# Strassen's products for the gate and up projections of MLP chunks 3 to 6, and another order at the start of the first head group

## The chip, the cores and the metric

The kernel runs on one core of a Trainium2 chip. The metric is device time in microseconds (us), as a median of three runs. TensorE (PE) does the matrix products, VectorE (DVE), ScalarE (ACT) and GpSimd (POOL) the elementwise work, and SyncE (SP) issues the transfers. Each engine works through its own instructions in order and waits on semaphores that the others raise.

## The reference

A decoder layer on x of 8 x 128 tokens of width 512, all in float32: a Mamba-2 block, then a gated MLP of inner width 1792, a layer norm, cross attention with 32 query heads in 8 groups, a layer norm, a mixture of low-rank adapters, and a last layer norm. The change touches the MLP,

```
h2 = rmsnorm(h, ln2_w)
mlp = silu(h2 @ gate_w.T) * (h2 @ up_w.T) @ down_w.T
```

and the start of the cross attention, `q = rmsnorm(x @ Wq.T)`, `k = rmsnorm(ctx @ Wk.T)`, softmax of `q k`, times `v`, times `Wo`.

## The kernel before

**Split operands.** A float32 operand is kept as two float32r parts, hi (a copy that ACT makes) and lo (the operand less hi, a subtraction by POOL for weights and by DVE for most activations). `mm3` (L509 to 513) makes each product of three matmuls: hi with hi, hi with lo, lo with hi. A 128 x 512 piece of output with K = 512 takes four K blocks, so 12 matmuls.

**The MLP.** The inner width is cut into seven chunks of 256 (c = 0 to 6; chunk 3 of the title is c = 2). Activations `act_hi` and `act_lo` lie transposed, 512 x 1024 tokens. A chunk has four steps `gu_step` (m = 0 to 3: two halves of 128 rows for each of two halves of 512 tokens), each with a gate product and an up product, 24 matmuls, into PSUM banks 2, 3 or 4, 5. Then:

- ACT: `silu` of the gate bank into `sg` (L1235).
- DVE: `hb = sg * up bank` (L2163). It waits until POOL has read the `hb` of two steps earlier (`hlo_done`), and PE starts a step only when the `hb` of two steps earlier is made (`h_done`).
- ACT: `h_hi` (L1243). POOL: `h_lo`.

After the four steps PE does eight down projections `dn_step` (one of 128 tokens each, 6 matmuls, banks 6 and 7). The first four need `h_lo` of steps 0 and 1, the last four that of steps 2 and 3 (`hlo_done`); from the third on each waits until DVE has added the bank of two earlier to the residual (`add_res` L2049, `o_add`). The hi and lo of the next chunk's gate and up weights (four pieces of 128 x 512: ACT `gu_hi` L1199, POOL `gu_rest`, through `lo` L1580) are made under the down projections. SP loads 1024 KB of them into `raw_a` when `gu_l` says that the old ones are split, and 512 KB of down weights into `raw_b`. All seven chunks have this form; chunks 2 to 5 are a loop on every engine.

Chunk 0 also holds the last norms and transposes (13 to 15). Chunk 1 holds six pieces of the context's split (ACT `ctx_split`, DVE `ctx_rest` through `lo` L1942, two behind each of the first three multiplications) and eight additions of x to the residual on POOL (`add_x` L1698: two, three and three behind `h_lo` 0, 1 and 2).

**The first head group.** Its slots take one block of 128 tokens each. The query projection of the next group is made by Strassen's seven products (`q_prod` L781, one in each slot) over the two halves of K and of the tokens, with sums of weights (POOL `combine_s`) and of tokens: t1, t2, t3, t4 are made raw, then hi by ACT (`t_round` L1342) and lo by DVE (`t_rest`). PE waits for the lo of a token sum by `t_lo`: product 1 for t3, product 2 for t2, product 3 for t1. In slot 1 DVE does `ot_rest`, `t_rest(t2)` and then `q_part`, which feeds the matmul `fold` of slot 2 (L806). Slot 0 begins on PE with `kv_step`, `s_step(0, 1)`, `q_step(1, 1)`.

The order of all this is written out by hand: each engine's program is a list of such calls.

Of the kernel before, what the change touches and what calls it, by code (L numbers as in the profile page):

```python
# [13 lines left out]
P = 128  # L14
# [15 lines left out]
def build_program(nc, x, ctx_t, mask, consts, fold_in, chan, rows, w_dt, w_in, w_out, w_gu, w_dn,  # L30
# [9 lines left out]
    with ctx:  # L40
# [76 lines left out]
        with ExitStack() as m:  # L117
            h_hi = sb(m, "h_hi", [P, 2, B * L], f32r)
            h_lo = sb(m, "h_lo", [P, 2, B * L], f32r)
            sg = sb(m, "sg", [P, 2, NTOK])  # L120
            hb = sb(m, "hb", [P, 2, NTOK])
            xre = sb(m, "xre", [P, B, DM])


        with ExitStack() as m:
# [30 lines left out]
            qpart = sb(m, "qpart", [P, 2, GH * 16])  # L156
            q2 = sb(m, "q2", [P, NTOK])
# [15 lines left out]
        t4_raw = [xn[:, k, :] for k in range(2)]  # L173
        p1_s = [w_raw[:, 0, 3072 + m * 512:3584 + m * 512] for m in range(2)]
# [76 lines left out]

        block = ctx.enter_context(nc.Block())
# [8 lines left out]
        WP_COL = [1024, 1536]  # L261
        A11, A12, A21, A22 = 0, 1, 2, 3
# [65 lines left out]
        def wo_turn(g, h):  # L328

            return 4 * g + ((h + 1) % 4 if is_last(g) else h) + 1  # L330

# [42 lines left out]
        def _(sp_eng):  # L374
# [48 lines left out]
            def next_mlp(c):  # L423

                sp_eng.wait_ge(dn_l, 2 * c + 2)
                sp_eng.dma_start(raw_b[:, 0:1024], w_dn[bass.ds(c + 1, 1)].rearrange("a p n -> (a p) n"))\
                    .then_inc(ld_dn, 16)
                sp_eng.wait_ge(gu_l, 4 * c + 4)
                sp_eng.dma_start(raw_a[:, :], w_gu[bass.ds(c + 1, 1)].rearrange("a p n -> (a p) n"))\
                    .then_inc(ld_gu, 16)  # L430

# [13 lines left out]
            with sp_eng.Fori(1, MLP_IT - 1) as c:  # L445
                next_mlp(c)

            sp_eng.wait_ge(gu_l, 4 * MLP_IT)
# [57 lines left out]
        def _(pe):  # L506
# [161 lines left out]
            def gu_step(c, k, n, turn=None):  # L668

                m_i = 2 * n + k  # L670
                pe.wait_ge(gu_l, 4 * c + 2 * k + 2)
                if not (isinstance(c, int) and 4 * c + m_i < 2):
                    pe.wait_ge(h_done, 4 * c + m_i - 1)
                tok = slice(n * NTOK, (n + 1) * NTOK)
                for which in range(2):
                    if which and turn is not None:
                        norm_t(turn, tb)
                    o = bank[(2, 4)[m_i % 2] + which]
                    for kk in range(KT):
                        c0 = GU_COL + (2 * k + which) * 512 + kk * P  # L680
                        t = mm3(o[:, :], w_hi[:, c0:c0 + P], w_lo[:, c0:c0 + P],
                                act_hi[:, kk, tok], act_lo[:, kk, tok], kk == 0, kk == KT - 1)
                t.then_inc(gu_mm, 1)

# [63 lines left out]
            with pe.Fori(2, MLP_IT - 1) as c:  # L748
                mlp_step(c)
# [114 lines left out]
            def slot(g, jj, make=True, before=True):  # L864
# [3 lines left out]
                turn = (g, jj + 1) if j < 3 else (pg, 4 * pn)  # L868
                if j == 3:
# [7 lines left out]
                if not before:  # L877
                    q_step(1, 1)
# [139 lines left out]
        def _(act):  # L1018
# [173 lines left out]
            def gu_hi(c, i):  # L1192

                act.wait_ge(ld_gu, 16 * c + 16)
                if isinstance(c, int) and c == 0:
                    act.wait_ge(in_mm, 20)
                else:
                    act.wait_ge(gu_mm, 4 * c)
# [32 lines left out]
            def silu(c, m_i):  # L1231
                act.wait_ge(gu_mm, 4 * c + m_i + 1)
# [20 lines left out]
            def mlp_step(c):  # L1253
# [23 lines left out]
                if not last:  # L1277
# [13 lines left out]
            def wq_hi(x):  # L1291
                act.wait_ge(ld_q, 16)
                act.wait_ge(*((o_mm, 8) if x < 2 else (gu_mm, 4 * MLP_IT)))
# [23 lines left out]
            with act.Fori(2, MLP_IT - 1) as c:  # L1317
                mlp_step(c)
# [68 lines left out]
            def slot(g, jj, make=True):  # L1387
# [46 lines left out]
                if start and jj == 0:  # L1434
                    wp_hi(1, 1)
                if start and jj == 1:
# [5 lines left out]
                part = part_late(g, jj)  # L1442
                if part and (make or jj < 3):
                    d, qn, qh = part
                    q_square(g + d, qn, qh)
# [129 lines left out]
        def _(pool):  # L1575
# [92 lines left out]
            def gu_rest(c, i):  # L1668
                pool.wait_ge(gu_h, 4 * c + i + 1)
# [30 lines left out]
            def mlp_step(c):  # L1700
                second, last = (isinstance(c, int) and c == x for x in (1, MLP_IT - 1))
                for m_i in range(4):
# [7 lines left out]
                    if second and m_i < 3:  # L1710
                        for b in ((0, 1), (2, 3, 4), (5, 6, 7))[m_i]:
                            add_x(b)
                    if last and m_i == 1:
# [4 lines left out]
                if not last:  # L1718
# [89 lines left out]
            with pool.Fori(2, MLP_IT - 1) as c:  # L1808
                mlp_step(c)
# [120 lines left out]
        def _(dve):  # L1930
# [225 lines left out]
            def mlp_step(c):  # L2156
                first, second, last = (isinstance(c, int) and c == x for x in (0, 1, MLP_IT - 1))
                for m_i in range(4):
                    dve.wait_ge(silu_done, 4 * c + m_i + 1)
                    dve.wait_ge(gu_mm, 4 * c + m_i + 1)  # L2160
# [13 lines left out]
                    if second and m_i < 3:  # L2174
                        ctx_rest(2 * m_i + 2)
                        ctx_rest(2 * m_i + 3)
                for b in range(B):
# [12 lines left out]

            mlp_step(0)
            mlp_step(1)
            with dve.Fori(2, MLP_IT - 1) as c:
                mlp_step(c)
# [128 lines left out]
            def slot(g, jj, make=True, before=True):  # L2323
# [51 lines left out]
                if start and jj == 1:  # L2375
                    t_rest(t2, t2_raw, 2, t_step, 12)
                if start and jj == 2:
                    t_rest(t1, t1_raw, 4, t_step, 8)
                if start and jj == 4:
                    t_rest(t4, t4_raw, 6, t_step, 14)  # L2380
                part = part_late(g, jj)
                if part and (make or jj < 3):
                    d, qn, qh = part
                    q_part(g + d, qn, qh)

# [229 lines left out]
```

## Time and profile before

| | |
|---|---|
| Median of three runs | 989.66 us (987.52 to 990.65) |
| Profiled execution | 986.14 us, of which 984.0 us are its span |
| MLP | about 133 to 364 us of the span |
| First head group begins | about 390 us |

Times in the rows count from the span's start. In a row of a timeline stand the start, the length, the engine, the line, what is written and read, the number of instructions, and in brackets how long the engine was idle before and what ended that. PE's matmuls overlap: the distance of two starts is what one costs, the length is its latency.

### The profile page before, as it was taken

What the parts mean: (1) busy time and instruction counts of PE and PEld (TensorE: products, weight loads), DVE (VectorE), ACT (ScalarE), POOL (GpSimd) and SP (SyncE); (2) the same over time, 40 slices, a digit from 0 to 9 for tenths busy, and PEclk for the clock granted to TensorE, in tenths of its full rate; (3) what the DMA queues carried; (4) which work ended last, traced back from release to release, by engine and by line L of the source; (5) the groups of instructions that cost most, each with busy time, mean ns of one, the idle gap of its engine ahead of it and who ended that gap; (6) DMA issues with size and microseconds to landing.
All of it is one profiled execution on the core that took longest, in us unless ns stands there. A gap on an engine that the chain in (4) does not pass through costs nothing.

```text
span 984.0 us, 15661 instructions
## 1 busy us (share of the span) xinstructions
PE 947.5 (96%) x4926; PEld 784.7 (80%) x4926; DVE 639.6 (65%) x1421; ACT 486.9 (49%) x1358; POOL 523.7 (53%) x432
## 2 busy tenths in 40 slices
PE   5998999999999999989999999999999999999896
PEld 3765688788888888878888888888888888888782
DVE  5755553513221357889778778768768778778877
ACT  5666442412231246645644654745645645555554
POOL 4346623834343456864674673673673764854323
PEclk9999999999999999999999999999999999999996
DMA  6200022310111111010110110110110120110002
GB/s 222 84 3 31 13 89 86 107 65 0 64 64 64 45 64 36 23 44 22 44 52 15 43 53 11 43 53 11 43 62 2 43 64 0 45 52 12 1 1 85
DMA packets 18024, 45.69 MB, mean 46 GB/s; under 512 B 2176, under 2 KB 2816, under 8 KB 16704
## 3 DMA queue, kind: packets, MB, share of 16 engines
q1 hardware_dynamic: 17984, 45.20, 13.7%
q8 instruction: 20, 0.33, 0.1%
q14 instruction: 20, 0.16, 0.1%
HBM read 43.10 MB, written 2.10 MB: 46 GB/s over the span
## 4 chain that ended last, share of the span: by engine, by line
PE 77%; POOL 7%; DVE 7%; issue 4%; ACT 2%; DMA 2%; SPq 0%; POOLq 0%; DVEq 0%; ACTq 0%
PE bank L511 22%; PE bank L513 22%; PE bank L512 22%; PE bank L828 4%; PE bank L838 2%; POOL w_lo L1580 2%; DMA raw_a<-in_w_q 1%; DVE pb L2299 1%; POOL res L1698 1%; PE bank L522 1%; POOL pb L1837 1%; PE bank L815 1%; POOL raw_a L1742 1%; PE bank L597 1%; DVE bst L2129 1%
## 5 line engine op out<-in xcount | busy, mean ns | idle before, releaser
L511 PE MATMUL bank<-act_hi,w_hi 128*128 128x512 f32 x448 | 182.7, 408 | 1.6 <-DVE act_lo L1942 1.6
L513 PE MATMUL bank<-act_hi,w_lo 128*128 128x512 f32 x448 | 175.3, 391 | 0.0
L512 PE MATMUL bank<-act_lo,w_hi 128*128 128x512 f32 x448 | 175.1, 391 | 0.0
L1837 POOL TENSOR_TENSOR pb<-pb,prec 128x512 f32<-128x512 f32 x64 | 66.8, 1044 | 163.1 <-DVE prec L2308 163.1
L1580 POOL TENSOR_TENSOR w_lo<-raw_a,w_hi 128x512 fp32r<-128x512 f32 x101 | 130.2, 1301 | 37.1 <-ACT w_hi L1302 21.6
L1371 ACT ACTIVATE pb<-pb,nmax 128x128 f32<-128x128 f32 x256 | 99.4, 391 | 46.5 <-DVE nmax L2303 46.5
L511 PE MATMUL bank<-w_hi,ot_hi 128*128 128x512 f32 x256 | 106.2, 415 | 1.1 <-DVE ot_lo L1942 0.6
L1580 POOL TENSOR_TENSOR h_lo<-hb,h_hi 128x512 fp32r<-128x512 f32 x28 | 37.3, 1333 | 120.5 <-ACT h_hi L1243 120.5
L511 PEld LDWEIGHTS bank<-act_hi,w_hi 128*128 128x128 f32 x448 | 84.7, 189 | 20.2 <-issue 4.1
L513 PE MATMUL bank<-w_hi,ot_lo 128*128 128x512 f32 x256 | 100.5, 393 | 0.0
L512 PE MATMUL bank<-w_lo,ot_hi 128*128 128x512 f32 x256 | 100.2, 391 | 0.0
L512 PEld LDWEIGHTS bank<-act_lo,w_hi 128*128 128x128 f32 x448 | 84.7, 189 | 18.0 <-issue 2.2
L513 PEld LDWEIGHTS bank<-act_hi,w_lo 128*128 128x128 f32 x448 | 84.4, 188 | 18.0
L2163 DVE TENSOR_TENSOR hb<-sg,bank 128x512 f32<-128x512 f32 x28 | 19.3, 688 | 115.8 <-ACT sg L1235 115.8
L1379 ACT ACTIVATE pt_hi<-bank 128x512 fp32r<-128x512 f32 x64 | 38.3, 598 | 105.5 <-PE bank L838 105.5
L1235 ACT ACTIVATE sg<-bank 128x512 f32<-128x512 f32 x28 | 16.8, 599 | 130.3 <-PE bank L513 130.3
L1580 POOL TENSOR_TENSOR w_lo<-raw_b,w_hi 128x512 fp32r<-128x512 f32 x56 | 72.1, 1306 | 7.1 <-ACT w_hi L1039 7.1
L511 PE MATMUL bank<-w_hi,ctx_hi 128*128 128x256 f32 x256 | 72.7, 284 | 0.0
L2299 DVE SCALAR_TENSOR_TENSOR pb<-bank,qr,mask_sb 128x128 f32<-128x128 f32 x256 | 71.5, 342 | 1.3 <-POOL qr L1825 1.2
L513 PE MATMUL bank<-w_hi,ctx_lo 128*128 128x256 f32 x256 | 71.6, 280 | 0.0
L512 PE MATMUL bank<-w_lo,ctx_hi 128*128 128x256 f32 x256 | 71.4, 279 | 0.0
L828 PE MATMUL bank<-k_t,q_t 128*128 128x128 f32 x512 | 67.7, 275 | 0.9 <-DVE pb L2299 0.8
(233 smaller groups left out, 2330.1 us busy)
## 6 DMA issues: line engine op xcount, KB each, us to landing
raw_a<-in_w_gu SPq DMA_DIRECT2D x7, 1024.0 KB, 5.3
raw_a<-in_w_q SPq DMA_DIRECT2D x28, 256.0 KB, 3.3
raw_b<-in_w_kv SPq DMA_DIRECT2D x8, 512.0 KB, 3.2
raw_b<-in_w_dn SPq DMA_DIRECT2D x7, 512.0 KB, 3.3
raw_b<-in_w_o SPq DMA_DIRECT2D x7, 512.0 KB, 4.9
raw_a<-in_w_o SPq DMA_DIRECT2D x14, 256.0 KB, 3.8
res<-in_x SPq DMA_DIRECT2D x8, 256.0 KB, 5.4
raw_b<-in_ctx_t SPq DMA_DIRECT2D x8, 256.0 KB, 3.0
```

The source lines that it names most:

```text
L511: mm(o, l_hi, r_hi, start=first, stop=False)
L512: mm(o, l_hi, r_lo, start=False, stop=False)
L513: return mm(o, l_lo, r_hi, start=False, stop=last)
L828: t = mm(bank[3][:, h * L:(h + 1) * L], q_t[:, n, h, tok], k_t[:, n, tok], start=True, stop=True)
L838: t = nc.tensor.transpose(bank[4][:, h * L:(h + 1) * L], pb[:, jj % 2, h, :], ident)
L1235: A(sg[:, m_i % 2, :], bank[(2, 4)[m_i % 2]][:, :], ACT.Silu).then_inc(silu_done, 1)
L1371: t = A(pb[:, jj % 2, h, :], pb[:, jj % 2, h, :], ACT.Exp, bias=nmax[:, jj % 2, h:h + 1], accum_out=psum_[:, jj % 2, h:h + 1])
L1379: A(pt_hi[:, :], bank[4][:, :], ACT.Copy).then_inc(pthi_done, 1)
L1580: TT(dst, src, f32(hi), ALU.subtract).then_inc(done, 1)
L1837: TT(pb[:, jj % 2, :, :], pb[:, jj % 2, :, :], prec[:, jj % 2, :].unsqueeze(2).to_broadcast([P, GH, L]), ALU.mult).then_inc(p_norm, 1)
L2163: TT(hb[:, m_i % 2, :], sg[:, m_i % 2, :], bank[(3, 5)[m_i % 2]][:, :], ALU.mult)\
L2299: t = STT(pb[:, jj % 2, h, :], bank[3][:, h * L:(h + 1) * L], qr[:, 4 * n + h, j:j + 1], mask_sb[:, :], ALU.mult, ALU.add)
```

## The change

- The four pieces of gate and up weights of a chunk are stored by halves of K: A11 and A12 (gate, K halves), A21 and A22 (up). Each `gu_step` of the chunks 0, 1 and 6 waits for all four.
- In chunks 2 to 5 PE makes seven products of 12 matmuls. Product 0 of a chunk stands ahead of the down projections of the chunk before. Banks are 2 to 5, 0 and 1.
- POOL makes four sums of weights for each of these chunks, and the lo of seven pieces in place of four. The second load of a chunk's weights (768 KB) waits for the lo of the last piece of the chunk before (`gl(c) + 7`).
- DVE makes 14 additions of a product to a running sum for each of these chunks; the multiplications read SBUF alone.
- The token sums t3 and g1 are made by POOL in chunk 0 (`gate_t3` behind the down weights' lo, `gate_t1` behind `h_lo` 2), t2 and half of t4 by DVE in chunk 1, and the rest in chunk 2.
- At the start of the first head group `q_square` (ACT) and `q_part` (DVE) stand ahead of the splits of token sums, `t_rest(t2)` goes to slot 2, and `q_step(1, 1)` goes to the head of slot 0.

In the diff, calls that follow one another are joined on a line, and words in brackets at the right are added.

```diff
+        def gl(c): 4 * c below c = 2, else 7 * c - 6        (gu_l, gu_h: weights split)
+        def gm(c): 4 * c below c = 2, else 14 * c - 20      (gu_mm: products done)
...
+            def next_fast(c):                               (SP)
+                sp_eng.wait_ge(gs_done, 4 * c + 4)
+                sp_eng.wait_ge(gu_l, gl(c) + 1)
+                load_g(c + 1)
+                sp_eng.wait_ge(dn_l, 2 * c + 2)
+                load_dn(c + 1)
+                sp_eng.wait_ge(gu_l, gl(c) + 7)
+                load_g_rest(c + 1)
...
-                pe.wait_ge(gu_l, 4 * c + 2 * k + 2)         (PE, gu_step)
+                pe.wait_ge(gu_l, gl(c) + 4)
...
+            def gate_prod(c, i):
+                pe.wait_ge(gu_l, gl(c) + i + 1)
+                if i == 0:
+                    pe.wait_ge(*((h_done, 8) if isinstance(c, int) and c == 2 else (ga_done, 12 * c - 22)))
+                elif i == 1:
+                    pe.wait_ge(h_done, 4 * c)
+                elif i == 3:
+                    pe.wait_ge(gc_done, 2 * c + 6)
+                elif i > 3:
+                    pe.wait_ge(ga_done, 12 * c - 14 + {4: 0, 5: 2, 6: 6}[i])
+                if isinstance(c, int) and c == 2 and i in (1, 2, 3, 6):
+                    pe.wait_ge(gt_lo, {1: 12, 2: 12, 3: 14, 6: 16}[i])
+                for m in range(2):
+                    for k in range(2):
+                        c0 = GU_COL + i % 4 * 512 + (2 * m + k) * P
+                        b_hi, b_lo = gate_rhs(i, k)
+                        t = mm3(bank[G_PAIR[i][m]][:, :], w_hi[:, c0:c0 + P], w_lo[:, c0:c0 + P], b_hi, b_lo,
+                                k == 0, k == 1)
+                    t.then_inc(gu_mm, 1)
+            def mlp_fast(c, more=True):
+                for i in range(1, 7):
+                    gate_prod(c, i)
+                if more:
+                    gate_prod(c + 1, 0)
+                for b in range(B):
+                    dn_step(c, b)
...
+                if not before:                              (PE, head of slot)
+                    q_step(1, 1)
...
+            def mlp_fast(c, more=True):                     (ACT)
+                A(gp1[m], bank[G_PAIR[0][m]][:, :], ACT.Copy).then_inc(gc_done, 1)     (m = 0, 1)
+                gb_hi(c, 4); dn_hi(c, 0); gb_hi(c, 5); dn_hi(c, 1); gb_hi(c, 6)
+                silu_fast(c, 0); silu_fast(c, 1); gb_hi(c + 1, 0)
+                h_split(c, 0); h_split(c, 1); silu_fast(c, 2); silu_fast(c, 3); gb_hi(c + 1, 1)
+                h_split(c, 2); h_split(c, 3); gb_hi(c + 1, 2); gb_hi(c + 1, 3)
...
+                    if first and m_i == 0:                  (POOL, mlp_step)
+                        gate_t3()
+                    if first and m_i == 2:
+                        gate_t1()
+            def gate_t3():                                  (gate_t1 alike: six operations)
+                for k in range(2):
+                    g_op(t3_raw[k], b21[k][1], b11[k][1], ALU.subtract, 0)
+                for k in range(2):
+                    g_op(t3_raw[k], t3_raw[k], b21[k][0], ALU.add, 9 + k)
+                for k in range(2):
+                    g_op(t3_raw[k], t3_raw[k], b11[k][0], ALU.subtract, 11 + k)
+            def gate_s(c):
+                pool.wait_ge(ld_g11, 16 * c)
+                pool.wait_ge(ld_gu, 16 * c + 16)
+                TT(gu_block(2), quad(A11), quad(A21), ALU.subtract).then_inc(gs_done, 1)
+                pool.wait_ge(gs_done, 4 * c + 1)
+                TT(gu_block(1), quad(A22), gu_block(2), ALU.subtract).then_inc(gs_done, 1)
+                TT(gu_block(3), quad(A21), quad(A22), ALU.add).then_inc(gs_done, 1)
+                TT(gu_block(4), quad(A12), gu_block(1), ALU.subtract).then_inc(gs_done, 1)
+            def mlp_fast(c, more=True):
+                gb_rest(c, 4); dn_rest(c, 0); gb_rest(c, 5); dn_rest(c, 1); gb_rest(c, 6)
+                gate_s(c + 1); gb_rest(c + 1, 0)
+                h_rest(c, 0); h_rest(c, 1); gb_rest(c + 1, 1)
+                h_rest(c, 2); h_rest(c, 3); gb_rest(c + 1, 2); gb_rest(c + 1, 3)
...
                     if second and m_i < 3:                  (DVE, mlp_step)
                         ctx_rest(2 * m_i + 2)
                         ctx_rest(2 * m_i + 3)
+                        if m_i == 0:
+                            gate_t2(0)
+                        elif m_i == 1:
+                            gate_t2(1)
+                            gate_lo(t3, t3_raw, 0)
+                        else:
+                            gate_t4(0)
+                            gate_lo(t2, t2_raw, 2)
...
+            def mlp_fast(c):                                (each gate_adds: 2 additions, of i = 3: 4)
+                for i in range(1, 5):
+                    gate_adds(c, i)
+                gate_mul(c, 0); gate_mul(c, 1); gate_adds(c, 5); gate_adds(c, 6)
+                gate_mul(c, 2); gate_mul(c, 3)
+                for b in range(B):
+                    add_res(8 + 8 * c + b, b, 6 + b % 2)
...
-                if start and jj == 1:                       (DVE, slot)
-                    t_rest(t2, t2_raw, 2, t_step, 12)
                 part = part_late(g, jj)
                 if part and (make or jj < 3):
                     d, qn, qh = part
                     q_part(g + d, qn, qh)
+                if start and jj == 2:
+                    t_rest(t2, t2_raw, 2, t_step, 12)
+                    t_rest(t1, t1_raw, 4, t_step, 8)
```

## Rows read from the trace of the kernel before

**Rows 1.** The page, part 1: busy time, share of the span, instructions.

```profile
PE 947.5 (96%) x4926; PEld 784.7 (80%) x4926; DVE 639.6 (65%) x1421; ACT 486.9 (49%) x1358; POOL 523.7 (53%) x432
```

**Rows 2.** Busy time by stretch, chunks 2 and 5: stretch, length, engines, PEclk, DMA share, GB/s.

```profile
200.50:233.20 32.70, 32.70 (x145) 26.99 (x145) 8.26 (x12) 8.05 (x14) 12.67 (x10) 1.00 0.13 49
...
298.70:331.50 32.80, 32.80 (x146) 27.08 (x145) 8.26 (x12) 8.05 (x14) 12.69 (x10) 1.00 0.16 55
```

**Rows 3.** The timeline of PE inside a gate product.

```profile
170.08 0.39 PE L512 MATMUL bank<-act_lo,w_hi 128*128 128x512 f32 x1
170.31 0.39 PE L513 MATMUL bank<-act_hi,w_lo 128*128 128x512 f32 x1
```

**Rows 4.** The timeline of POOL in chunk 0.

```profile
142.33 2.54 POOL L1580 TENSOR_TENSOR w_lo<-raw_b,w_hi 128x512 fp32r<-128x512 f32 x2
...
158.41 1.30 POOL L1580 TENSOR_TENSOR h_lo<-hb,h_hi 128x512 fp32r<-128x512 f32 x1 [4.14 <-ACT h_hi L1243]
159.66 5.06 POOL L1580 TENSOR_TENSOR w_lo<-raw_a,w_hi 128x512 fp32r<-128x512 f32 x4
```

**Rows 5.** The timeline of ACT, end of chunk 0: silu, h_hi, weights' hi.

```profile
156.34 0.60 ACT L1235 ACTIVATE sg<-bank 128x512 f32<-128x512 f32 x1 [2.41 <-PE bank L513]
157.70 0.63 ACT L1243 ACTIVATE h_hi<-hb 128x512 fp32r<-128x512 f32 x1 [0.76 <-DVE hb L2163]
```

**Rows 6.** The timeline of DVE in chunk 1.

```profile
176.35 3.28 DVE L1942 TENSOR_TENSOR ctx_lo<-raw_b,ctx_hi 128x512 fp32r<-128x512 f32 x2 [2.26 <-ACT ctx_hi L1250]
...
181.45 1.14 DVE L1942 TENSOR_TENSOR ctx_lo<-raw_b,ctx_hi 128x512 fp32r<-128x512 f32 x1 [1.22 <-ACT ctx_hi L1250]
...
189.72 0.69 DVE L2163 TENSOR_TENSOR hb<-sg,bank 128x512 f32<-128x512 f32 x1 [0.79 <-ACT sg L1235]
...
191.91 0.69 DVE L2049 TENSOR_TENSOR res<-res,bank 128x512 f32<-128x512 f32 x1 [0.69 <-PE bank L513]
...
196.92 0.69 DVE L2049 TENSOR_TENSOR res<-res,bank 128x512 f32<-128x512 f32 x1 [1.58 <-PE bank L513]
```

**Rows 7.** The timeline of POOL in chunk 1, beside the first row above.

```profile
176.08 3.00 POOL L1580 TENSOR_TENSOR w_lo<-raw_b,w_hi 128x512 fp32r<-128x512 f32 x2
```

**Rows 8.** DVE, first head group: two operations on SBUF with nothing like them on POOL.

```profile
429.19 1.28 DVE L1942 TENSOR_TENSOR act_lo<-act_raw,act_hi 128x512 fp32r<-128x512 f32 x2
```

**Rows 9.** The page, part 6: issues, KB each, median us to landing.

```profile
raw_a<-in_w_gu SPq DMA_DIRECT2D x7, 1024.0 KB, 5.3
...
raw_b<-in_w_dn SPq DMA_DIRECT2D x7, 512.0 KB, 3.3
```

**Rows 10.** The timeline of PE around the fold of slot 2.

```profile
424.92 0.43 PE L806 MATMUL bank<-qpart,fold 128*128 128x64 f32 x2 [2.54 <-DVE qpart L2220]
...
427.68 0.78 PE L511 MATMUL bank<-t,w_hi 128*128 128x512 f32 x1
428.25 0.61 PE L512 MATMUL bank<-t,w_hi 128*128 128x512 f32 x1
428.68 0.42 PE L513 MATMUL bank<-t,w_lo 128*128 128x512 f32 x1
```

**Rows 11.** Busy time by stretch: after that idle time, and after another.

```profile
82.00:86.00 4.00, 3.95 (x16) 2.67 (x15) 2.49 (x4) 3.83 (x9) 3.77 (x4) 1.00 0.00 0
...
425.00:429.00 4.00, 3.84 (x13) 3.06 (x14) 3.93 (x11) 3.04 (x8) 1.41 (x2) 0.57 0.00 0
```

**Rows 12.** PE's idle time ahead of the first of those stretches.

```profile
81.05 0.67 PE L597 MATMUL bank<-att,xtok 128*128 128x512 f32 x1 [2.12 <-DVE yb L2043]
```

**Rows 13.** The timeline of DVE in slots 1 and 2.

```profile
414.74 0.69 DVE L1942 TENSOR_TENSOR ot_lo<-bank,ot_hi 128x512 fp32r<-128x512 f32 x1 [0.64 <-ACT ot_hi L1385]
417.05 2.36 DVE L1942 TENSOR_TENSOR t<-t_raw,t 128x512 fp32r<-128x512 f32 x2 [1.62 <-POOL xn L1793]
...
424.18 0.69 DVE L2220 TENSOR_REDUCE qpart<-q2t 128x16 f32<-128x512 f32 x1
...
428.58 0.69 DVE L1942 TENSOR_TENSOR ot_lo<-bank,ot_hi 128x512 fp32r<-128x512 f32 x1
```

**Rows 14.** The timeline of PE in slot 0.

```profile
393.02 1.13 PE L828 MATMUL bank<-k_t,q_t 128*128 128x128 f32 x8 [0.75 <-DVE pb L2299]
```

More of the change, by code:

```diff
@@ L1276, in mlp_step @@
                         wkv_hi(0, 1)
-                if not last:
+                    if second and m_i == 0:
+                        t_round_g(t3, t3_raw, gt_pool, 13)
+                    if second and m_i == 2:
+                        t_round_g(t2, t2_raw, gt_dve, 15)
+                if first:
+                    for i in range(4):
+                        gu_hi(1, i)
+                if second:
+                    gb_hi(2, 0)
+                    gb_hi(2, 1)
+                    act.wait_ge(x_add, 8)
+                    t_round_g(g1, g1_raw, gt_pool, 19)
+                    gb_hi(2, 2)
+                    gb_hi(2, 3)
@@ new lines, in silu_fast @@
+            def silu_fast(c, x):
+                m, n = x % 2, x // 2
+                act.wait_ge(ga_done, 12 * c - 10 + 2 * n + m + 1)
+                gate = (gu2, gp1)[n][m]
+                A(gate, gate, ACT.Silu).then_inc(silu_done, 1)
+            def mlp_fast(c, more=True):
+                peeled = isinstance(c, int) and c == 2
+                for m in range(2):
+                    act.wait_ge(gu_mm, gm(c) + m + 1)
+                    act.wait_ge(h_done, 4 * c)
+                    if peeled:
+                        act.wait_ge(x_add, 8)
+                    A(gp1[m], bank[G_PAIR[0][m]][:, :], ACT.Copy).then_inc(gc_done, 1)
+                gb_hi(c, 4)
+                dn_hi(c, 0)
+                gb_hi(c, 5)
+                dn_hi(c, 1)
+                gb_hi(c, 6)
+                if peeled:
+                    act.wait_ge(cx_l, 8)
+                    t_round_g(t4, t4_raw, gt_dve, 19)
+                silu_fast(c, 0)
+                silu_fast(c, 1)
+                if more:
+                    gb_hi(c + 1, 0)
+                h_split(c, 0)
+                h_split(c, 1)
+                silu_fast(c, 2)
+                silu_fast(c, 3)
+                if more:
+                    gb_hi(c + 1, 1)
+                h_split(c, 2)
+                h_split(c, 3)
+                if more:
+                    gb_hi(c + 1, 2)
+                    gb_hi(c + 1, 3)
+                else:
@@ L1700, in mlp_step @@
             def mlp_step(c):
-                second, last = (isinstance(c, int) and c == x for x in (1, MLP_IT - 1))
+                first, second, last = (isinstance(c, int) and c == x for x in (0, 1, MLP_IT - 1))
                 for m_i in range(4):
@@ L1717, in mlp_step, with g_op, gate_t3 @@
                         wkv_rest(0, 1)
-                if not last:
+                if first:
+                    for i in range(4):
+                        gu_rest(1, i)
+                if second:
+                    gate_s(2)
+                    for i in range(4):
+                        gb_rest(2, i)
+            def g_op(o, x, y, op, seen):
+                if seen:
+                    pool.wait_ge(gt_pool, seen)
+                TT(o, x, y, op).then_inc(gt_pool, 1)
+            def gate_t3():
+                pool.wait_ge(n_lo, 12)
+                for k in range(2):
+                    g_op(t3_raw[k], b21[k][1], b11[k][1], ALU.subtract, 0)
+                for k in range(2):
+                    g_op(t3_raw[k], t3_raw[k], b21[k][0], ALU.add, 9 + k)
+                for k in range(2):
+                    g_op(t3_raw[k], t3_raw[k], b11[k][0], ALU.subtract, 11 + k)
```

224 lines of the change are left out of this document (186 added, 38 removed).

## The prediction

> **What bounds the kernel now.** I read the page's first part, then the busy time by stretch, then the timelines of the MLP engine by engine. PE is busy for 96% of the span [rows 1]. In chunks 2 and 5 it is busy for the whole stretch, at PEclk 1.00, and the two between are alike; POOL works 12.7 of 32.7 us there, DVE 8.3 [rows 2]. A chunk is 96 + 48 = 144 matmuls in 32.75 us, so one costs 0.227 us, which is the distance of two starts [rows 3] and not the 0.39 us of a record. So PE's instruction count sets the time, as long as nobody makes PE wait; the question is whether the added work does.
>
> **What goes.** Seven products of 12 matmuls replace 96: 12 fewer in each of four chunks, 48 x 0.227 = 10.9 us off PE.
>
> **What comes, unit prices.** A POOL operation on 128 x 512 costs 1.26 us in a row of four (5.06 / 4) [rows 4]. ACT takes 0.60 to 0.63 [rows 5]. DVE takes 0.69 where one input is a PSUM bank [rows 6], whatever POOL does. With both inputs in SBUF it takes 0.64 while POOL rests (1.28 / 2) [rows 8], but 1.64 beside POOL (3.28 / 2) [rows 6], and POOL's two then take 3.00 in place of 2.54: each such DVE operation holds POOL up by 0.46 [rows 4, 7]. It looks as if they take turns: DVE waits for the POOL operation in progress. A lone one takes 1.14 [rows 6].
>
> The Trainium skill says so in so many words ("SBUF — State Buffer", section "SBUF: two separate sides"): the port pair is an exclusive lock, held for a whole instruction, against DVE operations with two SBUF inputs. The trace agrees (1.64 against 0.64). By that rule every sum that the change puts on DVE while POOL has a queue costs one POOL operation more; by the row of a resting POOL it would be free of this, which is the first rival.
>
> **Chunk 0 (POOL's sums).** The lo of the down weights ends at 144.9 [rows 4]. Then `gate_t3` takes 6 x 1.26 = 7.6 (to 152.4), `h_lo` 1 and 2 take 2.5 (155.0), `gate_t1` 7.6 (162.5), the two context subtractions of DVE hold it up by 2 x 0.46 (163.4), and `h_lo` 3 ends at 164.7 instead of 159.7. PE ends its products at 156.3 [rows 5] and wants `h_lo` 3 for the fifth down projection, 4 x 6 x 0.229 = 5.5 later, at 161.8. So PE stands for 2.9 us; behind it are four down projections and all of chunk 1. The lo of chunk 1's weights (5.06 from 164.7) is ready at 169.8 while PE ends at 170.2, so the wait for all four pieces costs nothing more. Everything is now 2.8 us late. Bounds: 2.0 if DVE's two don't disturb, 3.5.
>
> **Chunk 1 (DVE's sums and splits).** DVE's context subtractions grow from 6 to 16 operations on SBUF: four behind the first multiplication, six behind the second, six behind the third, and the next multiplication stands behind them. POOL has 3, 4 and 4 operations in these stretches. In the chunk's new time:
> - The first block begins at 176.35 + 2.8 = 179.15, takes 4 x 1.64 = 6.6, and the second multiplication ends at 186.4.
> - Then ACT rounds h and a piece of context, a gap of 1.3 (1.22 in [rows 6]), then four operations beside POOL and two without: 6.6 + 1.3; the third multiplication ends at 196.2.
> - The same again: the fourth ends at 206.1, against 190.4 + 2.8 = 193.2.
> - DVE's first additions to the residual come after it; the third down projection waits for the first of them, to 206.8. Some first operations of a block come free at once (the 1.14), so I take 0.9 off: 205.9.
>
> PE would begin that third projection at 191.9 + 2.8 = 194.7, where its second ends (in the kernel before DVE's second addition starts at 191.91) [rows 6]. It stands for 11.2 us, with six projections behind it. In the kernel before, it waited 0.9 there for POOL (1.58 in place of 0.69 between two additions [rows 6]); that goes. Net 10.3. Bounds: with 0.64 for all 16 it is 0 (the blocks fit into a step of 5.4), with 1.64 for all 12.5.
>
> **Chunks 2 to 5 (the handover to the next chunk's product 0).** PE reaches it after six products: 6 x 12 x 0.227 = 16.3 us after product 1 begins. What it waits for: product 2 ends at 5.4; ACT's hi and POOL's lo of piece 6 take 0.63 + 1.26, with the hand-overs 7.6. Only then SP issues 768 KB; 512 KB land in 3.3 us and 1024 KB in 5.3 [rows 9], so 4.3: 11.9. Then POOL makes four sums and the lo of the piece, 5 x 1.26 = 6.3: 18.2, and DVE's two multiplications, which now read SBUF alone, hold it up by 0.9: 19.1. PE stands for 2.8 us; queued behind are product 0 and eight down projections. `h_lo` 0 to 3 follow at POOL in time. Three handovers have this (2 to 3, 3 to 4, 4 to 5). The first is later by 0.8, because POOL comes late out of chunk 1 and DVE has six more operations on SBUF. Sum 9.2. Bounds: 0.2 each (a load that lands after 2.7, and no lock) to 4.4. DVE's 14 additions, 0.69 each, fit between the products (2.7 for 2 or 4 of them), and ACT's 19 operations too.
>
> **PE's clock.** After 2.54 us without work (and 0.16 more) the matmul starts lie 0.43 apart until 428.7 [rows 10]; PEclk is 0.57 over 425 to 429, half clock (1.2 of 2.4 GHz) for 3.4 us [rows 11], a loss of 1.7. After 2.12 us idle [rows 12] it stayed at 1.00 [rows 11]. The five new waits are 2.9, 11.2, 3.6, 2.8, 2.8. The long one surely pays 1.7; I give the four others 0.7 each, between 0 and 1.7. Sum 4.5; bounds 0 and 8.5.
>
> The Trainium skill describes this case ("TensorE: Matmul & The Clock Gate", section "HAM oscillation — how this bites in real kernels"): a loop that waits in each round drops the clock in each round. By it all five pay, 8.5 and not 4.5, the third rival; the row of 2.12 us speaks against it for the short ones.
>
> **Start of the first head group.** `q_part` no longer stands behind `t_rest(t2)`: it can follow `ot_rest` (ends 415.4) where it followed the split (ends 419.4) [rows 13], so the fold's 2.54 us go. But `t_rest(t2)` is now behind `ot_rest` of slot 2, and product 2 waits for it. Moved forward by the 3.9 us that DVE gains, `ot_rest` stands at 424.7 in place of 428.58, and t2's lo is ready at 425.3 + 1.28 = 426.6. PE, without the fold's wait and at full clock, is there at 423.5: it stands for 3.1 us in the next place, and its clock falls there as before. It began product 2 at 427.68 [rows 10] and begins it at 426.6, but runs more of it at half clock. I take -0.5; bounds 0 and -5 (no new wait). In slot 0 PE's 0.75 us go [rows 14], but `kv_step` 1 still waits for DVE's copy of k; 0, bounds 0 and -0.7.
>
> **The sum**, against the profiled 986.14 us: -10.9 + 2.9 + 10.3 + 9.2 + 4.5 - 0.5 = +15.5, so 1001.6. That execution was 3.5 us below the median of 989.66; from the median it is 1005.2. I predict 1005.
>
> **Rivals.**
> 1. *POOL and DVE keep ahead: faster.* The place is the shared path of POOL and DVE; the price is the 0.46 and 1.0 of each meeting. It decides at 0.64 us for DVE's operations on SBUF: then chunk 1 has no stop, each handover costs 1.8 and chunk 0 costs 2.0: -10.9 + 2.0 - 0.9 + 5.4 - 0.5 = -5.0, about 985. For it: DVE is busy only 65% and POOL 53% [rows 1]. Against it: the 1.64 beside POOL. Chance 0.11.
> 2. *The pile-up in chunk 1 is half of mine*, because DVE's operations meet POOL less: at the lone 1.14 to 1.2 in place of 1.64, 12 operations give back 5.5, and a shorter wait is kinder to the clock: +9, about 999. Chance 0.17.
> 3. *The clock falls at each wait*: +4 more, about 1009. Chance 0.14.
> 4. My forecast: 0.52. Between the first two lies a rest of 0.06, in which the sums cancel (about 990), from handovers that land early.
>
> The likeliest's own range is 1000 to 1011. The range of 8 in 10 is 992 to 1013: it takes in the second and the third. A measurement of this kernel tells 0.3% (3 us) from no change. Faster than 986.7: 0.11; within: 0.06; slower than 992.6: 0.83.
>
> **What would show it.** On PE's timeline: a stop ahead of the fifth down projection of chunk 0 (released by `h_lo`); one of about 11 us ahead of the third of chunk 1 (by DVE's addition to the residual); one at each product 0, released by `w_lo`, with POOL's first weight sum right behind the landing of the load; DVE's subtractions and sums in chunk 1 at 1.6 us each; PEclk below 1.00 behind the waits; and at the head group a wait at product 2 in place of the fold's. My forecast falls if DVE's 16 operations take under 1 us each, or if the 768 KB land before 10 us after product 1 begins.

## The result, and the profile after

The changed kernel takes 1010.35 us (median of 4, 1006.07 to 1014.53), the kernel before beside it 989.53: ratio 1.021, interval 1.019 to 1.023, so it is slower, by about 2%. Predicted were 1005 us, range 992 to 1013. The profiled execution took 1008.71 us, against 986.14; its sum was predicted as 1001.6. I count chunks from 0, as the prediction does.

The page's part 1 of the kernel after, to [rows 1]: POOL worked 56 us more, DVE 59 us more, and PE has 48 matmuls fewer. PE's busy time is the same to 0.1 us all the same: from the start of the MLP to that of the first head group it is 3.1 us less, where half clock and a longer pitch (the distance of two starts) take back most of what the 48 matmuls gave, and before the MLP it is 3.0 us more (below).

```profile
PE 947.4 (94%) x4878; PEld 781.0 (78%) x4878; DVE 698.6 (69%) x1493; ACT 501.6 (50%) x1386; POOL 580.1 (58%) x472
```

PE's waits of the kernel after over 120 to 400 us (the MLP; what PE waited for: us in total, times, longest):

```profile
PE bank L563 <- DVE res L2297: 11.6, 3, 11.0
PE bank L563 <- POOL w_lo L1743: 9.6, 3, 3.5
PE bank L563 <- POOL h_lo L1743: 2.8, 1, 2.8
```

And where they stand, in PE's timeline (start, length, then the idle time before it). In order: the fifth down projection of chunk 0, the third of chunk 1, product 0 at three handovers, the fold and product 2 of the first head group, which answer to [rows 10]:

```profile
167.63 0.50 PE L563 MATMUL bank<-w_hi,h_hi 128*128 128x512 f32 x1 [2.75 <-POOL h_lo L1743]
...
209.38 0.76 PE L563 MATMUL bank<-w_hi,h_hi 128*128 128x512 f32 x1 [11.02 <-DVE res L2297]
...
242.69 0.50 PE L563 MATMUL bank<-act_hi,w_hi 128*128 128x512 f32 x1 [3.45 <-POOL w_lo L1743]
...
276.45 0.49 PE L563 MATMUL bank<-act_hi,w_hi 128*128 128x512 f32 x1 [3.08 <-POOL w_lo L1743]
...
310.16 0.79 PE L563 MATMUL bank<-act_hi,w_hi 128*128 128x512 f32 x1 [3.07 <-POOL w_lo L1743]
...
445.23 0.33 PE L899 MATMUL bank<-qpart,fold 128*128 128x64 f32 x2
...
450.11 0.76 PE L563 MATMUL bank<-t,w_hi 128*128 128x512 f32 x1 [3.37 <-issue]
```

Look at the lengths too: a record of 0.76 to 0.79 behind a wait is a matmul at half clock, one of 0.47 to 0.50 at full clock. The stretches say the same (start:end, length, PE busy, PEclk, DMA share, GB/s):

```profile
204.00:212.00 8.00, 2.62 (x6) 0.50 0.00 0
...
310.00:316.00 6.00, 5.84 (x14) 0.50 0.00 0
...
276.00:284.00 8.00, 7.55 (x33) 1.00 0.10 33
```

DVE in chunk 1, to [rows 6]. The pairs L2451 and L2458 are token sums beside POOL's additions; L2190 `t<-t_raw,t` is a low part while POOL rests. After them the additions to the residual (L2297) come, on which PE waited 11.02. The last line is POOL's, two additions of x beside the first pair: 1.72 each, where 1.26 is its price undisturbed:

```profile
185.69 3.48 DVE L2451 TENSOR_TENSOR t_raw<-t_raw,act_hi 128x512 f32<-128x512 f32 x2
...
190.98 3.07 DVE L2190 TENSOR_TENSOR ctx_lo<-raw_b,ctx_hi 128x512 fp32r<-128x512 f32 x2 [1.22 <-ACT ctx_hi L1343]
193.97 3.49 DVE L2451 TENSOR_TENSOR t_raw<-t_raw,act_lo 128x512 f32<-128x512 f32 x2
197.39 1.28 DVE L2190 TENSOR_TENSOR t<-t_raw,t 128x512 fp32r<-128x512 f32 x2
...
203.43 3.41 DVE L2458 TENSOR_TENSOR xn<-act_hi,t_raw 128x512 f32<-128x512 f32 x2
...
208.56 1.27 DVE L2297 TENSOR_TENSOR res<-res,bank 128x512 f32<-128x512 f32 x2
```

```profile
185.17 3.44 POOL L1861 TENSOR_TENSOR res<-res,xre 128x512 f32<-128x512 f32 x2
```

POOL at the first handover: it sits idle until the load lands, then makes the weight sums and only then the low part for which PE waits (L1743 at 241.36):

```profile
236.09 1.50 POOL L1925 TENSOR_TENSOR w_raw<-raw_a 128x512 f32<-128x512 f32 x1 [5.80 <-DMA raw_a<-in_w_gu]
...
240.14 1.27 POOL L1930 TENSOR_TENSOR w_raw<-raw_a,w_raw 128x512 f32<-128x512 f32 x1
241.36 1.27 POOL L1743 TENSOR_TENSOR w_lo<-raw_a,w_hi 128x512 fp32r<-128x512 f32 x1
242.58 2.55 POOL L1743 TENSOR_TENSOR h_lo<-hb,h_hi 128x512 fp32r<-128x512 f32 x2
```

### The profile page after: what moved, and what is told of

Same layout as the page of the kernel before. It is cut to its first block, busy times and chain, and to the rows that moved or that the text cites. A ratio compares the mean times of both kernels' runs of the same rounds, so it can differ in the third digit from the quotient of the medians.

```text
span 1006.9 us, 15750 instructions
## 1 busy us (share of the span) xinstructions
PE 947.4 (94%) x4878; PEld 781.0 (78%) x4878; DVE 698.6 (69%) x1493; ACT 501.6 (50%) x1386; POOL 580.1 (58%) x472
## 4 chain that ended last, share of the span: by engine, by line
PE 72%; POOL 8%; DVE 8%; issue 5%; DMA 2%; ACT 2%; SPq 0%; POOLq 0%; DVEq 0%; ACTq 0%
PE bank L563 21%; PE bank L565 20%; PE bank L564 20%; PE bank L921 4%; POOL w_lo L1743 3%; PE bank L931 2%; DMA raw_a<-in_w_q 1%; PE bank L574 1%; DVE pb L2629 1%; POOL t_raw L1897 1%; PE bank L624 1%; DVE t_raw L2451 1%; PE bank L908 1%; PE bank L649 1%; DVE bst L2377 1%
## 5 line engine op out<-in xcount | busy, mean ns | idle before, releaser
L563 PE MATMUL bank<-act_hi,w_hi 128*128 128x512 f32 x368 | 154.4, 419 | 11.4 <-POOL w_lo L1743 9.6
L1743 POOL TENSOR_TENSOR w_lo<-raw_a,w_hi 128x512 fp32r<-128x512 f32 x97 | 125.5, 1301 | 40.6 <-ACT w_hi L1463 19.7
L565 PE MATMUL bank<-act_hi,w_lo 128*128 128x512 f32 x368 | 146.0, 397 | 0.0
L564 PE MATMUL bank<-act_lo,w_hi 128*128 128x512 f32 x368 | 145.9, 397 | 0.0
L563 PEld LDWEIGHTS bank<-act_hi,w_hi 128*128 128x128 f32 x368 | 70.7, 192 | 28.9 <-issue 11.8
L1743 POOL TENSOR_TENSOR w_lo<-raw_b,w_hi 128x512 fp32r<-128x512 f32 x56 | 72.3, 1308 | 23.2 <-ACT w_hi L1299 14.6
L564 PEld LDWEIGHTS bank<-act_lo,w_hi 128*128 128x128 f32 x368 | 70.7, 192 | 15.5 <-issue 2.4
L565 PEld LDWEIGHTS bank<-act_hi,w_lo 128*128 128x128 f32 x368 | 70.5, 191 | 15.5
L2297 DVE TENSOR_TENSOR res<-res,bank 128x512 f32<-128x512 f32 x64 | 43.7, 685 | 40.1 <-PE bank L565 39.9
L2190 DVE TENSOR_TENSOR ot_lo<-bank,ot_hi 128x512 fp32r<-128x512 f32 x64 | 44.2, 691 | 34.3 <-ACT ot_hi L1548 33.8
L921 PEld LDWEIGHTS bank<-k_t,q_t 128*128 128x128 f32 x512 | 64.1, 192 | 2.1 <-issue 0.5
```

What stands on the lines that cost most here:

```text
L563: mm(o, l_hi, r_hi, start=first, stop=False)
L564: mm(o, l_hi, r_lo, start=False, stop=False)
L565: return mm(o, l_lo, r_hi, start=False, stop=last)
L921: t = mm(bank[3][:, h * L:(h + 1) * L], q_t[:, n, h, tok], k_t[:, n, tok], start=True, stop=True)
L1743: TT(dst, src, f32(hi), ALU.subtract).then_inc(done, 1)
L2190: TT(dst, src, f32(hi), ALU.subtract).then_inc(done, 1)
```

## The experiments

Theory: the change makes PE wait in places of its own, each with its own cause: POOL's order at the handovers, the lock between DVE and POOL in chunk 1, the place of t2's low part in the head group; the products themselves save what was counted. Rivals: the engines' load as such is the bound, so that a wait removed comes back elsewhere. The expectations below count chunks from 1: their "chunk 2" is chunk 1 here, their "chunks 4, 5 and 6" are 3, 4 and 5.

**head_alone.** The kernel before with the head group's part of the change only:

```
 DVE:  - if start and jj == 1: t_rest(t2, ...)      (ahead of q_part)
       + if start and jj == 2: t_rest(t2, ...)      (behind q_part)
 ACT:  q_square ahead of t_round;  PE: q_step(1, 1) first in slot 0
```

> The kernel before with the change of the first head group alone: the norm's piece ahead of the splits of the token sums, both of those in slot 2. Theory: in the profile after, the fold's wait of 2.54 us is gone and a wait of 3.37 us stands at product 2 with the clock at half speed behind it, and from the fold matmul to the end the two kernels took 597.55 and 597.46 us. So the time stays within 0.5 us of before (989.5), and TensorE's wait at product 2 is about 3.4 us. Rival: the exchange saves its 2.5 us and the wait at product 2 comes from the MLP's change (its t2 block and stack): then this kernel is 2 to 3 us faster than before and product 2 starts without a wait.

Measured: 987.38 us (median of 12) against 989.47; ratio 0.9984, interval 0.9973 to 0.9994, so 1.6 us faster by the ratio, 0.6 to 2.7 (2.1 by the medians). The wait at product 2 is there without any of the MLP's change, and the half clock follows it, here from the third matmul on (429.26):

```profile
428.73 0.47 PE L511 MATMUL bank<-t,w_hi 128*128 128x512 f32 x1 [3.37 <-issue]
```

```profile
429.00:433.00 4.00, 4.00 (x12) 0.57 0.02 4
```

The exchange of one wait for the other is shown; the gain is about 1 us more than the 0.5 expected, for which no run shows a cause.

**head_t2_early.** The same, with t2's low part in slot 1 behind `q_part`:

```
-if start and jj == 2:
+if start and jj == 1:
     t_rest(t2, t2_raw, 2, t_step, 12)
+if start and jj == 2:
     t_rest(t1, t1_raw, 4, t_step, 8)
```

> The kernel before with the same change, but VectorE's low part of t2 stands directly behind the norm's piece of slot 1, not in slot 2. Theory: what holds product 2 is that low part alone, queued behind slot 2's softmax; placed here it costs the piece nothing, so both waits go (2.5 us at the fold, 3.4 us at product 2 and the 2 to 3 us of half clock behind it): 3 to 6 us faster than before, no wait of over 0.5 us at product 2. Rival: VectorE is full in slots 1 and 2, so two more operations of 0.7 us each here push the softmax and the wait appears at the next scores or transposes: within 1 us of before.

Measured: 984.53 us against 989.47; ratio 0.9949 (0.9935 to 0.9963), 5.0 us faster. PE's waits over 380 to 440 us have lost the 3.4; 0.7 is left at the fold, in a line that head_alone does not have. The first matmul of product 2 has no idle time before it, and PEclk stays at 1.00 in the stretch around it:

```profile
PE bank L806 <- DVE qpart L2220: 0.7, 1, 0.7
```

```profile
428.47 0.47 PE L511 MATMUL bank<-t,w_hi 128*128 128x512 f32 x1
```

```profile
427.00:431.00 4.00, 3.84 (x19) 1.00 0.00 0
```

So it was t2's place that made the wait.

**pool_order.** The kernel after with POOL's order in chunks 2 to 5 changed (and ACT's `gb_hi(c + 1, 1)` behind its `h_split`s):

```
+gb_rest(c + 1, 0)
+for x in range(4):
+    h_rest(c, x)
 gate_s(c + 1)
-gb_rest(c + 1, 0)
-h_rest(c, 0); h_rest(c, 1)
 gb_rest(c + 1, 1)
-h_rest(c, 2); h_rest(c, 3)
```

> The kernel after, with POOL's order in chunks 3 to 6 changed: the low part of block A11 and the four low parts of h ahead of the four weight sums, the low parts of the summed blocks behind them (ScalarE's order likewise). Theory: the three waits of TensorE at product 0 of chunks 4, 5 and 6 (3.45, 3.08, 3.07 us) are the wait for the low part of A11, which stood behind 5.3 us of weight sums that begin only when the DMA has landed; the waits go, none of over 0.5 us takes their place, and the time falls by 9.6 us and up to 2.9 us of clock, to 997 to 1001 us. Rival: POOL's total per chunk is the bound, and the waits come back at product 1 (its block is now made last) at 2 us or more each: 1003 to 1010 us.

Measured: 996.83 us, 13.5 less than the kernel after. The line of `w_lo` is gone from PE's waits over 120 to 400 us, nothing took its place, and all else is as it was:

```profile
PE bank L563 <- DVE res L2293: 11.6, 3, 11.0
PE bank L563 <- POOL h_lo L1742: 2.8, 1, 2.8
...
```

POOL does the same work as in the kernel after; its load was not the bound, its order was. The three waits were 9.6 us. The other 3.9, by the medians, I put down to the clock behind them; that is not shown in full (in the profile after one of the three waits cost 2.8 of clock), and it is more than the 2.9 expected.

**sums_from_psum.** The kernel after, with one SBUF operand of DVE's ten added operations in chunk 1 replaced by a PSUM bank. Number, size and order of the operations stay; the sums themselves are left out, here and in the next kernel, so the results are not the layer's:

```
-TT(t2_raw[k], (t3_raw, t2_raw)[part][k], b12[k][part], ALU.add)
+TT(t2_raw[k], bank[k][:, :], b12[k][part], ALU.add)
 ... (t4's first difference and the low parts of t3 and t2 alike)
```

> The kernel after, but VectorE's ten added token operations of chunk 2 (t2, t4 and the low parts of t3 and t2) read one operand from a PSUM bank in place of SBUF; their values are then not those of the sums. Theory (the lock): an operation with two SBUF operands of VectorE waits for POOL's and takes 1.7 us beside it against 0.65 alone; with one PSUM operand each takes 0.69 us, the ten take 6.9 in place of 12.9 us, and the wait of 11.0 us at the third down projection of chunk 2 falls to 3 us or less; POOL's operations beside them fall from 1.7 to 1.3 us; the time falls by 8 to 10 us, to 1000 to 1003. Rival (the count): ten more operations and their waits on ScalarE's high parts are too many for the chunk whatever each takes; the wait stays at 7 us or more.

Measured: 1004.86 us (998.77 to 1007.44), 5.5 less than the kernel after and above the 1000 to 1003 expected; the wait fell from 11.0 to 4.9, between the two forecasts. In its profile the clock fell to half behind all five waits, in that of the kernel after behind two, so the time says less here than the wait.

```profile
PE bank L563 <- DVE res L2297: 5.5, 3, 4.9
```

DVE's timeline shows what was left. The sums take 0.64 each, but the context subtractions, old operations with both operands in SBUF, still take 1.5 beside POOL:

```profile
189.95 3.08 DVE L2190 TENSOR_TENSOR ctx_lo<-raw_b,ctx_hi 128x512 fp32r<-128x512 f32 x2 [1.22 <-ACT ctx_hi L1343]
192.95 1.28 DVE L2451 TENSOR_TENSOR t_raw<-bank,act_lo 128x512 f32<-128x512 f32 x2
```

**all_from_psum.** So those six read a bank too (`raw_b` replaced by `bank[i % 2]` in `ctx_rest` for i of 2 and more).

> As the kernel whose ten token operations read a PSUM bank, and VectorE's six context subtractions of chunk 2 read one there too (values again not those of the reference). There the wait at the third down projection fell from 11.0 to 4.9 us, and the subtractions still took 1.5 to 1.6 us each beside POOL's additions of x. Theory (the lock is all of it): sixteen operations of 0.64 us fit, a quarter of the chunk then holds 0.7 + 1.2 + 6 x 0.64 = 5.7 us of VectorE for 5.4 us of TensorE, and the wait falls to 0 to 1.5 us. Rival (the count and the hand-overs with ScalarE carry what was left): 3.5 to 5 us stay.

Measured: 995.48 us, 14.9 less than the kernel after. The wait on DVE is gone, with all sixteen operations in their places:

```profile
PE bank L563 <- POOL w_lo L1743: 10.5, 3, 4.2
PE bank L563 <- POOL h_lo L1743: 2.8, 1, 2.8
PE bank L563 <- DVE res L2297: 0.6, 2, 0.4
```

```profile
182.97 1.29 DVE L2190 TENSOR_TENSOR ctx_lo<-bank,ctx_hi 128x512 fp32r<-128x512 f32 x2 [2.26 <-ACT ctx_hi L1343]
```

POOL's pairs beside them take 2.55, not 3.0 to 3.44 (its down weights 2.55 and first two additions of x 2.55):

```profile
185.21 2.55 POOL L1861 TENSOR_TENSOR res<-res,xre 128x512 f32<-128x512 f32 x2
```

So the 11 us need the meetings of DVE's and POOL's operations on SBUF: the same sixteen operations without them leave 0.4. They need the ten added operations too, because the six old ones met POOL in the kernel before and made no such wait. Freeing the ten alone removed 6.1; the rest stood in six operations that the change had not touched and had only crowded. Of the 14.9 us, 11.0 are the wait; the clock behind it had cost 2.1.

**both_orders.** The kernel after with pool_order's and head_t2_early's edits.

> The kernel after with both reorderings that have run: POOL's order in chunks 3 to 6, and the low part of t2 behind the norm's piece in slot 1. Theory (each wait is its own): the times add, 996.8 less the 5.0 by which the early low part was faster than before and the 1.6 that the head's change alone already gave counted once, so 992 to 994 us; what is left over the kernel before are the waits of 2.8 us in chunk 1 and 11.0 us in chunk 2, with the clock behind them. Rival: the head group's wait is hidden behind another there, and the time stays at 996 to 998.

Measured: 991.86 us, ratio to before 1.0028 (1.0016 to 1.0041); PE's long waits are 11.0 and 2.7. The wait at product 2 is gone too, so each repair works beside the other. The time is 2.1 us below what the medians of the single runs add up to (996.83 less the 2.85 between head_alone and head_t2_early: 993.98), just under the range expected. That is not the repairs' doing as far as the profiles show: in code that neither edit touches, up to the wait in chunk 0, this execution was already 2.75 us ahead of pool_order's (165.22 against 167.97).

**three_chunks_spread.** Both repairs, Strassen in chunks 3 to 5 only, and the token sums spread:

```
-G_FAST = (2, MLP_IT - 2)
+G_FAST = (3, MLP_IT - 2)
 POOL: t3 in chunk 0;  gate_t1() behind gu_rest at the end of chunk 1
 DVE, chunk 2: gate_t2(0), gate_t2(1) ahead of the first multiplication;
               gate_lo(t3), gate_t4(0), gate_lo(t2) behind the first, second, third
```

> Strassen for chunks 4 to 6 only, both reorderings kept, and the token sums spread: t3 on POOL in chunk 1, g1 on POOL at the end of chunk 2, VectorE's t2 ahead of chunk 3 and the low part of t3, t4 and the low part of t2 one pair in each quarter of chunk 3, where both engines idle more than half the time. Theory: with no wait behind the sums the matmuls' price is all that is left: 989.5, less 5.0 (the head group), less 36 matmuls of 0.227 us (8.2), plus about 1.1 for the longer pitch of the products of sums: 975 to 980 us, no wait of TensorE over 1 us in chunks 1 to 6. Rival: the meetings of POOL and VectorE cost wherever the sums stand, and waits of 3 us or more appear in chunk 2 or 3: 982 to 988 us.

Measured: 976.07 us; ratio 0.9869 (0.9852 to 0.9886). That is 13.1 us faster than the kernel before and 34 faster than the kernel after. Not all of it is Strassen's: the head group's edit alone gave 5.0 (head_t2_early), three chunks of 2.39 (below) give 7.2. The longest of PE's waits over 120 to 400 us:

```profile
PE bank L567 <- DVE kraw L2404: 1.0, 1, 1.0
PE bank L567 <- POOL h_lo L1747: 0.6, 1, 0.6
```

It also gives the products' price without waits. From the first down projection of one Strassen chunk to that of the next:

```profile
257.83 0.39 PE L567 MATMUL bank<-w_hi,h_hi 128*128 128x512 f32 x1
...
288.19 0.39 PE L567 MATMUL bank<-w_hi,h_hi 128*128 128x512 f32 x1
```

30.36 us against 32.75 before, so 2.39 saved in a chunk and not 12 x 0.227 = 2.72.

**four_chunks_spread.** Both repairs and all four Strassen chunks, with the sums in chunks 0 and 1:

```
 POOL: gate_t1() behind gu_rest at the end of chunk 0
 DVE:  gate_t2(0) in chunk 0's third quarter; gate_t2(1), gate_t4(0) from its sixth addition on;
       gate_lo(t2) behind chunk 1's last two additions; gate_lo(t3) beside product 0
```

> Strassen for chunks 3 to 6 as in the kernel after, both reorderings kept, and the token sums spread over chunks 1 and 2: g1 on POOL behind the weights of chunk 2, t2 and t4's first half on VectorE in and behind chunk 1's additions, the low parts of t2 and t3 among the last additions of chunk 2 and beside product 0. Theory: the same operations cost TensorE nothing where the engines idle: 989.5 less 5.0, less 48 x 0.227 = 10.9, plus 1.5 for the pitch: 972 to 978 us, and neither the wait of 2.8 us in chunk 1 nor that of 11.0 us in chunk 2. Rival: VectorE's additions hold the down projections' banks, each extra operation of up to 1.7 us beside them stalls TensorE, 1 to 2 us at four to six places: 978 to 985 us, slower than the version with three chunks.

Measured: 977.59 us; ratio 0.9886 (0.9869 to 0.9902). Neither large wait is there. Four of 0.5 to 0.8 are, 2.5 us in all, while POOL rests for only 0.8 us between 167.7 and 218:

```profile
198.12 0.50 PE L563 MATMUL bank<-w_hi,h_hi 128*128 128x512 f32 x1 [0.61 <-POOL h_lo L1741]
...
204.50 0.50 PE L563 MATMUL bank<-act_hi,w_hi 128*128 128x512 f32 x1 [0.61 <-POOL w_lo L1741]
...
213.76 0.47 PE L563 MATMUL bank<-g_hi,w_hi 128*128 128x512 f32 x1 [0.46 <-DVE g_lo L2184]
...
223.10 0.47 PE L563 MATMUL bank<-t_hi,w_hi 128*128 128x512 f32 x1 [0.83 <-issue]
```

They are as much as the 2.4 us that the fourth chunk saves, and the time is level with that of three chunks (the intervals overlap). It is within the 972 to 978 expected, but short stops such as the rival named are there.

**four_chunks_later_x.** To remove the first two of them:

```
-for b in ((0, 1), (2, 3, 4), (5, 6, 7))[m_i]: add_x(b)       (m_i < 3)
+for b in ((0, 1), (2, 3, 4), (), (5, 6, 7))[m_i]: add_x(b)
+gb_rest(2, 0)
 gate_s(2)
```

> The version with four chunks spread, with POOL's last three additions of x of chunk 2 behind the last low part of h (not ahead of it), and the low part of block A11 ahead of chunk 3's weight sums. Theory: the waits of 0.6 us for that low part of h and of 0.6 us for A11's go, those for VectorE (0.5 at product 3, 0.8 at product 6) stay: 976.2 to 976.8 us, level with the version with three chunks (976.1). Rival: POOL's queue from the last low part of h to product 3 is full, so that what goes at the first places comes back at product 1 and 2: 977 to 979 us.

Measured: 978.88 us (976.92 to 979.42), and the rival is right: both waits went, and one of 2.8 appeared at product 1, with the half clock behind it. Its low part stands behind the weight sums, which now stand behind the three additions of x:

```profile
207.94 0.56 PE L563 MATMUL bank<-t,w_hi 128*128 128x512 f32 x1 [2.81 <-POOL w_lo L1741]
```

In this place POOL is nearly full: it rested 0.78 us and 1.89 us between 167 and 218, the 1.89 ahead of the last `h_lo` (193.87), where those additions had stood. That its load alone is the bound here is not shown, since that rest and the slower operations beside DVE (1.75 and 1.72 for the last two weight sums) delay the same low part; no order tried here with four Strassen chunks had neither.

## Why the prediction was right

The terms between the start of chunk 0's products and the first matmul that reads `qpart` (at 386.45 in the kernel before, 409.44 after), where the kernel after took 273.48 us and the kernel before 253.57, 19.9 more. The last row of the table lies behind that stretch. A wait's own value is taken from PE's timeline:

| term | predicted | measured |
| --- | --- | --- |
| 48 matmuls | -10.9 | -10.9, but +1.3 by the longer pitch |
| chunk 0, `h_lo` 3 | +2.9 | 2.75 |
| chunk 1, third down projection | 11.2, net +10.3 | 11.02, net 10.1 |
| three handovers | 3.6 + 2.8 + 2.8 | 3.45 + 3.08 + 3.07 |
| clock behind the five waits | +4.5 | +4.9, at two places |
| rest, by difference; no run shows its causes | 0 | about +2 |
| first head group | -0.5 | -1.6 (-0.6 to -2.7), head_alone; -0.1 between the two profiles |

The waits stood in the places named, each term's size came within 0.4 us, and each was shown by an edit of its own or by its going away. The sizes owe something to luck, inside the handovers above all. What was off:

- **The pitch of the products.** I priced all products at 0.227. The ones with a token sum as operand run at 5.60 / 24 = 0.233, as the starts of products 1, 3 and 4 in the kernel after show; 0.33 us a chunk. The step "what goes" was too large by 1.3 us.

```profile
222.42 0.40 PE L563 MATMUL bank<-t,w_hi 128*128 128x512 f32 x1
...
228.02 0.39 PE L563 MATMUL bank<-g_hi,w_hi 128*128 128x512 f32 x1
...
230.82 0.39 PE L563 MATMUL bank<-act_hi,w_hi 128*128 128x512 f32 x1
```

- **Inside the handovers.** The 2.8 us is a sum of four steps, and each was off. Counted from the start of product 1, SP issued the 768 KB at 8.0 (predicted 7.6). They took 5.6, 5.2 and 4.9 us until POOL began, not 4.3; the profile's median from issue to landing is

```profile
raw_a<-in_w_gu SPq DMA_DIRECT2D x3, 768.0 KB, 5.2
```

  The weight sums and the low part took 6.5, 6.6 and 6.9, not 7.2, with less meeting of DVE than priced. PE arrived after 16.8, not 16.3, by the longer pitch. The errors cancel to 3.08 and 3.07 for the predicted 2.8. The first handover's extra, predicted as 0.8 and measured as 0.4, had another cause: POOL did not come late out of chunk 1 (piece 6's low part began 6.6 us after product 1 did, against 6.5 in the later chunks), the load took longer.
- **Where the clock falls.** The sum was right, its distribution was not: 11.02 cost 2.1 and the last 3.07 cost 2.8, the other three nothing. The third rival, that every wait pays, is wrong for this execution; in the profile of sums_from_psum all five did (2.74, 4.90, 3.19, 3.13 and 3.06 us; behind the first, half clock from the fifth matmul on).
- **Before the MLP.** In code that the change does not touch, the profiled execution was already 3.1 us later than the one before, some 1.4 of it behind the 2.12 us of idle time that stayed at full clock in [rows 11, 12] and here did not. Its PE row, and then PEclk over the 4 us from 82 on (third column from the right):

```profile
82.71 1.10 PE L649 MATMUL bank<-att,xtok 128*128 128x512 f32 x2 [2.12 <-DVE yb L2291]
```

```profile
82.00:86.00 4.00, 3.29 (x7) 1.77 (x8) 3.16 (x5) 3.98 (x6) 2.11 (x2) 0.74 0.00 0
```

  These 3.1, the pitch's 1.3, the rest's 2 and the head group's 0.4 make most of the 7 us by which the profiled 1008.71 lies above the sum of 1001.6. The first three were not in the prediction's sum; the range was wide enough to take them in.
- **The working inside chunk 1.** The 11.2 came out of 1.64 for most of sixteen operations. In the trace those beside POOL took 1.5 to 1.74, and the last pair of the second and of the third block, with POOL at rest, 0.64. A little more and a little less cancelled; the first rival (0.64 for all) is what all_from_psum makes real, and there the wait is indeed 0.4. The upper bound of 12.5 for "1.64 for all" is a slip: four operations more at 1.64 in place of 0.64 give 11.2 + 4.0 = 15.2.

The Trainium skill's rule that I weighed ("SBUF — State Buffer", section "SBUF: two separate sides") held: with a PSUM operand DVE no longer met POOL, 0.64 in place of 1.5 to 1.7. Of the clock, the Trainium skill ("TensorE: Matmul & The Clock Gate", section "HAM oscillation — how this bites in real kernels") describes a loop whose waits of about 3 to 5 us drop the clock in each round. The prediction read from it that all five waits pay, the three that it priced below 3 us too, which is more than the section says. Two of five did in the profile after, one of them behind 3.07 us, while 3.45 us kept the full clock; in that of sums_from_psum all five did.

## What to carry to other kernels

Removing instructions from the engine that bounds is paid for by work on others, and what decided here was mostly where that work is queued and not how busy those engines are over the whole: POOL at 58% and DVE at 69% cost 23 us of waits, and the same work in other places 2.5. Before moving sums to DVE and POOL, count per stretch the operations with all operands in SBUF on both, the old ones too, and price them as one shared queue; give one operand in PSUM where that can be. What the bounding engine needs first must stand first in the helper's queue, ahead of work that is merely due, and the order must follow each need: two edits of order were worth 18.5 of the 34 us between the slowest and the fastest version.

## What was not expected of the hardware

**The same idle time, another clock.** PE's waits at the handovers are of nearly one length in three kernels: 3.45, 3.08, 3.07 (after), 4.17, 3.25, 3.07 (all_from_psum), 3.19, 3.13, 3.06 (sums_from_psum). By the first matmul behind each (0.77 to 0.80 or 0.47 to 0.50) the clock was at half behind 3.07 alone in the first kernel, behind 4.17 and 3.25 in the second, behind all in the third. The two waits of 3.07, at the same handover, show both, and so do the waits in chunk 0, 2.75 at full clock behind it in the first kernel and 2.76 at half clock in the second: PEclk behind the first 3.07 stands above (310 to 316), and this is the stretch of the second's:

```profile
301.00:305.00 4.00, 3.59 (x16) 1.00 0.00 0
```

A fall cost 2.1 to 2.8 us in the kernel after. Its four executions, at mean clocks of 0.979, 0.981, 0.971 and 0.972, took 1008.7, 1006.1, 1014.5 and 1012.0 us; the version without waits spread by 2.7. What decides whether the clock falls after some 3 us I can't tell from these runs.

**A DVE operation that waited for a whole queue.** Mostly DVE and POOL took turns (1.74 each, both slowed). Once, in three_chunks_spread, DVE's first sum lasted from 203.84 to 210.35, 6.51 us, until the last of six POOL operations was through (it began during the second), and those were not slowed (1.29 to 1.31 each):

```profile
203.84 6.51 DVE L2454 TENSOR_TENSOR t_raw<-t_raw,act_hi 128x512 f32<-128x512 f32 x1
```

```profile
203.53 1.30 POOL L1901 TENSOR_TENSOR q2t<-act_lo 128x512 f32<-128x512 f32 x1
...
208.52 1.29 POOL L1901 TENSOR_TENSOR q2t<-q2t,act_hi 128x512 f32<-128x512 f32 x1
```

PE did not wait for it. Why it went that way and not in turns stays open.
